# A gated cross-attention block: what follows the attention on groups of 128 rows across batches

## What is computed

```python
def xattn(hidden, ctx, mask, ...):            # per batch: hidden 100x256, ctx 1444x256
    q, k, v = hidden @ Wq.T + bq, ctx @ Wk.T + bk, ctx @ Wv.T + bv   # 16 heads of 16
    scores = clip(q @ k.T / 4, -50, 50); scores = where(mask, scores, -50)
    probs = softmax(scores); ctx = probs @ v
    delta = rs * (ctx @ Wo.T + bo)
    return layernorm(delta) * gamma + beta

def ffn(x, w1, w2, w3):                       # aq: rows to 8 bits, wq: weights to -1, 0, 1
    h = silu(aq(x) @ wq(w1).T) * (aq(x) @ wq(w2).T)
    return aq(h) @ wq(w3).T

x = x + tanh(g_xattn) * xattn(layernorm(x), ctx_2048, mask, ...)
x = x + tanh(g_ffn) * ffn(layernorm(x), w1, w2, w3)
```

## Time and profile before

| | us |
|---|---|
| median of 3 runs | 1345.64 (1344.66 to 1347.27) |
| the profiled execution's own span | 1347.5 |
| TensorE busy in it | 1303.3 |
| VectorE | 1114.3 |
| ScalarE | 964.8 |
| GpSimd | 443.3 |
| one batch in the middle | 40.0 |

### The profile page before, as it was taken

The page is one execution under the profiler, slowest core; times in us unless marked ns, Lnnn a source line. Parts: engine busy times, 40 slices in busy tenths (PEclk is TensorE's granted clock), DMA queues, the critical chain, the costliest instruction groups (busy, mean ns, idle before and its releaser), DMA issues.

```text
span 1347.5 us, 48025 instructions
## 1 busy us (share of the span) xinstructions
PE 1303.3 (97%) x19984; PEld 1207.4 (90%) x19984; DVE 1114.3 (83%) x2248; ACT 964.8 (72%) x1617; POOL 443.3 (33%) x751
## 2 busy tenths in 40 slices
PE   5999999999999999999999999999999999999993
PEld 4988999999999999999999999999999999999982
DVE  5878888888888888888888888888888888888864
ACT  3776777677777777777777777767777777777761
POOL 3323333323334322333332334332333332333310
PEclk9999999999999999999999999999999999999985
DMA  8867677667777767777767767766767776767630
GB/s 227 195 154 169 162 187 169 161 166 171 164 185 174 166 164 168 173 169 178 168 164 174 173 157 187 173 162 164 174 154 191 172 166 165 173 165 177 148 74 9
DMA packets 142511, 222.15 MB, mean 165 GB/s; under 512 B 29194, under 2 KB 135630, under 8 KB 142286
## 3 DMA queue, kind: packets, MB, share of 16 engines
q1 hardware_dynamic: 128632, 198.78, 61.3%
q0 software_dynamic: 12288, 19.69, 6.7%
q10 hardware_dynamic: 1366, 0.53, 0.2%
HBM read 54.00 MB, written 3.28 MB: 43 GB/s over the span
## 4 chain that ended last, share of the span: by engine, by line
PE 89%; SPq 4%; DVE 3%; DMA 2%; issue 1%; ACT 1%; POOL 0%; DVEq 0%; POOLq 0%
PE sc L1239 22%; PE pvb L1259 20%; PE cb L1294 19%; PE cb L1280 18%; SPq L309 4%; PE mb L1351 3%; PE mb L1320 2%; PE mb L1329 2%; DMA k_st<-k_lo 2%; PE mb L1366 2%; PE mb L1358 1%; DMA c_in<-in_ctxT 0%; PE mb L1313 0%; DVE c_hi L754 0%; PE mb L1335 0%
## 5 line engine op out<-in xcount | busy, mean ns | idle before, releaser
L556 ACT ACTIVATE e_sb<-sc 121x800 f32<-121x800 f32 (+1 forms) x768 | 645.6, 847 | 147.9 <-PE sc L1239 135.3
L1239 PE MATMUL sc<-q_st,k_st 96*121 96x200 f32 (+1 forms) x3072 | 472.2, 276 | 7.1 <-issue 3.0
L1239 PEld LDWEIGHTS sc<-q_st,k_st 96*121 96x121 f32 (+1 forms) x3072 | 411.6, 185 | 34.6 <-issue 8.5
L793 DVE TENSOR_SCALAR e_sb<-e_sb,hi_b 121x1600 f32<-121x1600 f32 (+1 forms) x384 | 399.6, 1048 | 0.8 <-ACT e_sb L556 0.8
L1259 PE MATMUL pvb<-e_sb,v_sb 121*32 121x100 f32 x12288 | 287.6, 251 | 0.0
L1259 PEld LDWEIGHTS pvb<-e_sb,v_sb 121*32 121x32 f32 x12288 | 266.3, 110 | 22.2 <-issue 19.0
L1294 PE MATMUL cb<-wv_hi,c_hi 128*121 128x256 f32 (+1 forms) x768 | 222.1, 289 | 1.6 <-DVE k_lo L784 1.3
L784 DVE SCALAR_TENSOR_TENSOR k_lo<-cb,bk_c,k_hi 128x484 fp32r<-128x484 f32 (+1 forms) x192 | 134.5, 700 | 107.5 <-ACT k_hi L568 107.5
L1294 PE MATMUL cb<-wv_hi,c_lo 128*121 128x256 f32 (+1 forms) x768 | 216.1, 281 | 0.0
L1294 PE MATMUL cb<-wv_lo,c_hi 128*121 128x256 f32 (+1 forms) x768 | 216.0, 281 | 0.0
L470 POOL DMA_DIRECT2D q_st<-bd_hi x256 | 164.0, 644 | 123.7 <-DVE bd_lo L839 120.7
(11 more groups left out here) (160 smaller groups left out, 1508.5 us busy)
## 6 DMA issues: line engine op xcount, KB each, us to landing
k_st<-k_hi SPq DMA_DIRECT2D x512, 121.0 KB, 2.9
c_in<-in_ctxT SPq DMA_DIRECT2D x64, 484.0 KB, 4.0
k_st<-k_lo SPq DMA_DIRECT2D x256, 121.0 KB, 2.9
k_st<-k_hi SPq DMA_DIRECT2D x256, 119.0 KB, 3.5
c_in<-in_ctxT SPq DMA_DIRECT2D x32, 476.0 KB, 4.7
k_st<-k_lo SPq DMA_DIRECT2D x128, 119.0 KB, 3.2
q_st<-bd_hi POOLq DMA_DIRECT2D x256, 50.0 KB, 3.3
q_st<-bd_lo POOLq DMA_DIRECT2D x128, 50.0 KB, 3.3
```

The source lines that it names most:

```text
L556: nc.scalar.activation(e_sb[e_slot(b, n)][0:TL[n], k * SW:(k + 1) * SW].rearrange("p (o c) -> p o c", o=2), sc[q % NSC][0:TL[n], :, 0:2 * PW],
L793: V.tensor_scalar(e, e, E_LO, hi_b[b.par][0:TL[n], n:n + 1], ALU.max, ALU.min).then_inc(clip_done, 1)
L1239: last = T_.matmul(sc[q % NSC][0:TL[n], e // 2, (e % 2) * PW:(e % 2 + 1) * PW], k_st[st_slot(b, n // TPC)][:, pr // NQ, pr % NQ, t0:t0 + T ...
```

## The change

The rows of all batches are taken as one array of 3200 rows, cut into 25 groups of 128. `full_group(b)` gives the group whose last rows are batch b's, or nothing for the seven batches that complete none. The softmax division of each batch writes its 100 columns of oT into a ring of 256 columns (in two pieces where they wrap); the first half of the attention's reading goes to a tile pT of its own. Every step behind that (`delta` to `result`) runs once per group, at the tile at which it ran before, in the batch behind the one that completes the group, on 128 partitions, with `gd` and `ge` in place of the batches d and b-2. x_res gets its 128 rows by a load of its own from x (`load_res`, SP's queue), and beta is added in place by GpSimd. The transposes of x2 and h read 128 rows. The count of steps of the attention's own part moves to a new semaphore (`A_V`). `load_x` waits for xn instead of the addition of beta. The general pass is written out batch by batch in place of its hardware loops.

The core of the diff; renamed or widened tiles of the same kind, the general pass's calls and repeated forms are left out:

```diff
+    NG = NB * S // P
+    RING = 2 * P
...
-        x_res = [sb(f"x_res{i}", [S, H]) for i in range(2)]
+        x_res = [sb(f"x_res{i}", [P, H]) for i in range(2)]
...
-        zt, oT = sb("zt", [P, KT, S]), sb("oT", [P, KT, S])
+        zt, pT, oT = sb("zt", [P, KT, S]), sb("pT", [P, KT, S]), sb("oT", [P, KT, RING])
...
+        def full_group(b):
+
+            g = S * (b.row + 1) // P - 1
+            if b.row < 0 or g < S * b.row // P:
+                return None
+            return whole(g, NG if b.base else 0)
...
+        def ring(row, count):
+
+            start = row % RING
+            first = min(count, RING - start)
+            return [(0, slice(start, start + first))] + ([(first, slice(0, count - first))] if first < count else [])
+
+        x_rows, out_rows = x.rearrange("b s h -> (b s) h"), out.rearrange("b s h -> (b s) h")
...
-            def store(b):
-                sp.wait_ge(result_done, b.n + 1)
-                sp.dma_start(out[bass.ds(b.row, 1), :, :].rearrange("o s h -> (o s) h"), y_out[:, :]).then_inc(stored, 16)
+            def store(g):
+                sp.wait_ge(result_done, g.n + 1)
+                sp.dma_start(out_rows[P * g.row:P * (g.row + 1), :], y_out[:, :]).then_inc(stored, 16)
+
+            def load_res(g):
+                if g.row >= 2:
+                    sp.wait_ge(dve_post, D_V.after(g.plus(-2), "x1"))
+                elif g.base:
+                    sp.wait_ge(dve_post, D_V.after(whole(NG - 1), "x1"))
+                sp.dma_start(x_res[g.par][:, :], x_rows[P * g.row:P * (g.row + 1), :]).then_inc(res_loaded[g.par], 16)
...
                 if nxt2:
-                    sp.wait_ge(pool_x, X_P.after(b, "res"))
+                    sp.wait_ge(dve_x, X_V.after(b, "xn"))
                     load_x(b.plus(2))
+                if full_group(b):
+                    load_res(full_group(b))
                 if nxt:
                     sp.wait_ge(split_done, SPLIT.after(b.plus(1), "lo0"))
                     load_c(b.plus(1), 2)
-                if prev2:
-                    store(b.plus(-2))
+                if full_group(b.plus(-2)):
+                    store(full_group(b.plus(-2)))
                 stack_k(b, 2)
...
+            def residual(g):
+                pool.wait_ge(res_loaded[g.par], res_count(g))
+                if not g.base and g.row == 0:
                     pool.wait_ge(s_setv, SETV["beta"])
-                if older:
-                    pool.wait_ge(dve_post, D_V.after(b.plus(-2), "x1"))
-                nc.gpsimd.tensor_tensor(x_res[b.par][:, :], x_in[b.par][:, :], beta_t[0:S, :], ALU.add
-                                        ).then_inc(pool_x, 1)
+                alone()
+                nc.gpsimd.tensor_tensor(x_res[g.par][:, :], x_res[g.par][:, :], beta_t[:, :], ALU.add
+                                        ).then_inc(pool_res, 1)
...
             def attention_out(b):
-                d_wait(b, "rz")
-                dv(V.tensor_tensor(oT[:, :, :], oT[:, :, :], zs[:, :, :], ALU.mult))
+                a_wait(b, "rz")
+                for at, cols in ring(S * b.row, S):
+                    size = cols.stop - cols.start
+                    put = V.tensor_tensor(oT[:, :, cols], pT[:, :, at:at + size], zs[:, :, at:at + size], ALU.mult)
+                av(put)
...
-            def x_turn(b, user):
+            def x_turn(b, user, older):
                 pe.wait_ge(dve_x, X_V.after(b, "xn"))
                 if user:
                     pe.wait_ge(dve_post, D_V.after(user, "dl"))
+                elif older:
+                    pe.wait_ge(result_done, older.n + 1)
...
-                for k in range(KT):
-                    last = T_.matmul(mb[0:S, 0:H], oT[:, k, :], wo[:, k, :], start=k == 0, stop=k == KT - 1)
+                cols = slice(P * g.row % RING, P * g.row % RING + P)
                 for k in range(KT):
+                    last = T_.matmul(mb[:, 0:H], oT[:, k, cols], wo[:, k, :], start=k == 0, stop=k == KT - 1)
                 last.then_inc(pe_post, 1)
...
                 for k in range(KT):
-                    last = T_.transpose(mb16[:, k * S:(k + 1) * S], x2q[:, k * P:(k + 1) * P], identb[0:S, 0:S])
+                    last = T_.transpose(mb16[:, k * P:(k + 1) * P], x2q[:, k * P:(k + 1) * P], identb[:, :])
...
                 for k in range(FT):
-                    last = T_.transpose(mb16[:, k * S:(k + 1) * S], hq[:, k * P:(k + 1) * P], identb[0:S, 0:S])
+                    last = T_.transpose(mb16[:, k * P:(k + 1) * P], hq[:, k * P:(k + 1) * P], identb[:, :])
...
-                    if prev2 and n == 2:
-                        down(b.plus(-2))
+                    if ge and n == 2:
+                        down(ge)
                     if nxt:
                         if n == 4:
-                            x_turn(c, d if prev else None)
+                            x_turn(c, gd, ge)
                         if n == 5:
                             x_query(c)
-                    if prev:
+                    if gd:
                         if n == 3:
-                            delta(d, prev2)
+                            delta(gd, d)
...
-                            x2_turn(d)
+                            x2_turn(gd)
                         if n == 8:
-                            up(d, 0, 0)
+                            up(gd, 0, 0)
                         if n in (9, 10):
-                            up(d, n - 9, 1)
+                            up(gd, n - 9, 1)
                     attend()
-                    if prev2 and n == 1:
-                        h_turn(b.plus(-2))
-                    if prev and n == 9:
-                        up(d, 1, 0)
+                    if ge and n == 1:
+                        h_turn(ge)
+                    if gd and n == 9:
+                        up(gd, 1, 0)
```

More of the change, by code:

```diff
@@ L207, in flamingo_block @@
         stored = sem("stored")
+        res_loaded = [sem(f"res_loaded{i}") for i in range(2)]
+        pool_res, dve_att = sem("pool_res"), sem("dve_att")
         odd_known, care_known = sem("odd_known"), sem("care_known")
@@ L335, in _, with batch @@
             sp.dma_start(m_in[0:TL[-1], NT - 1, :], maskT[(NT - 1) * TT:T, :]).then_inc(s_mask, 16)
-            def batch(b, own, nxt, nxt2, prev2):
+            def batch(b, own, nxt, nxt2):
                 if own:
@@ L1188, in passes @@
                 for step in (first_sum, x1_stats, x1_aggr):
-                    step(e)
+                    step(last)
                 if not base:
@@ L1365, in down, with batch @@
                 for k in range(FT):
-                    last = T_.matmul(mb[0:S, 0:H], hT[:, k, :], w3q[:, k, :], start=k == 0, stop=k == FT - 1)
+                    last = T_.matmul(mb[:, 0:H], hT[:, k, :], w3q[:, k, :], start=k == 0, stop=k == FT - 1)
                 last.then_inc(pe_post, 1)
-            def batch(b, own, nxt, prev, prev2):
+            def batch(b, own, nxt, prev):
                 c, d = b.plus(1), b.plus(-1)
+                gd, ge = full_group(d), full_group(b.plus(-2))
                 first = not prev
@@ L1442, in passes @@
                         ctx_item(b, w, 1)
-                batch(whole(0, base), True, True, False, False)
-                batch(whole(1, base), True, True, True, False)
-                batch(whole(2, base), True, True, True, True)
-                if base:
-                    with pe.Fori(base // 2 + 1, (base + NB - 2) // 2) as i:
-                        batch(Batch(2 * i + 1, i, 1, base), True, True, True, True)
-                        batch(Batch(2 * i + 2, i + 1, 0, base), True, True, True, True)
-                else:
-                    for n in range(3, NB - 1):
-                        batch(whole(n), True, True, True, True)
+                for n in range(NB - 1):
+                    batch(whole(n, base), True, True, n > 0)
                 e = whole(NB - 1, base)
-                batch(e, True, False, True, True)
+                batch(e, True, False, True)
+                last = full_group(e)
                 for n in range(NT - VISIT, NT):
@@ L1457, in passes @@
                     pv(e, n, 1)
-                h_turn(e.plus(-1))
-                down(e.plus(-1))
-                delta(e, True)
+                h_turn(last.plus(-1))
+                down(last.plus(-1))
+                delta(last, e)
                 if not base:
```

325 lines of the change are left out of this document (151 added, 174 removed).

## The result

The changed kernel takes **1331.9 us** (median of four runs, 1329.4 to 1335.6), the kernel before 1346.0 beside it: a ratio of 0.990 with a 95% interval of 0.988 to 0.992. The profiled execution was the fastest of the four, 1329.4 us with a span of 1327.6 (a run's time is 1.8 us more than its span in every run here).

A forecast was written before the change was run, and what follows sets the result against it. The order of TensorE's instructions was taken to set the time. -21.0 + 2.4 + 0.4 + 2.5 + 0.5 + 2.8 = -12.4 us took the profiled 1347.5 to 1335.1, the median to 1333.2 us; range 1327 to 1340.

The forecast's parts named there:

- -21.0, what leaves TensorE: TensorE steps missing in the two batches behind each of seven that complete no group: 3.00 us per batch, -21.0 in all.
- +2.4, the wider turns: The eight turns per group on TensorE go from 100 to 128 moving columns: 0.10 us a group, +2.4 us.
- +0.4, the last group: In the last group, where all is in series, the wider turns and copies cost some +0.4 us.
- +0.5, the wrapped ring: Twelve batches whose columns wrap the 256-column ring get a second VectorE multiplication: +0.5 us (0 to 1.5).
- (1) +2.5, VectorE's list in b+2: Two batches behind each gap, TensorE waits 0.36 us for VectorE's k_lo before tile 7's v product: +2.5 us (0 to 6.2).
- (2) +2.8, the stacking of k in b+1: One batch behind each gap, TensorE waits 0.4 us for k_st copies before tile 0's scores: +2.8 us (0 to 8.0).
- rival B: No new stalls, as k_lo, q_st and copies may come earlier: 1327.4 us; sign: b+1 falls to 37.9; chance 0.20.
- The offset: The profiled execution stands 1.9 us over the runs' median (1345.64), so 1335.1 becomes a median of 1333.2 us.
- Rival A: The forecast itself, with its stalls between half and double: 1329 to 1338 us; chance 0.60.
- D: Rival: 25 extra 128 KB x_res loads delay the k_st copies in every group's batch: slower, 1350 us; chance 0.05.
- E: Rival: TensorE's stationary-column loads are no longer hidden, 10 us on top of the forecast: 1343 us, no change; chance 0.04.

The follow-up runs named there:

- Run 1: Changed kernel with TensorE repeating the missing group steps, unread, in six of seven places; other engines as in the changed kernel: 1349.5 us, ratio 1.0045 to the kernel before.
- run 8: Changed kernel without VectorE's 1.40 us reciprocal of the softmax sums in the seven batches b+2: 1329.7 us, ratio 0.9897 to the kernel before.
- run 5: Changed kernel with the turns of x2 and h and ScalarE's copies of them back at 100 rows and columns: 1331.8 us, ratio 0.9903.
- run 6: Changed kernel with the last six of twelve copies of each batch's first key chunk issued by GpSimd instead of SyncE: 1536.1 us, ratio 1.143.
- run 9: Changed kernel without the body of the general pass, flag still read: 1330.8 us, ratio 0.989 to the kernel before.
- run 10: Changed kernel with GpSimd issuing the eight rounded-part query copies first, the four of the remainder behind them: 1325.8 us, ratio 0.9852.
- run 3: Changed kernel with queries (q_st) copied for the first two batches only, later batches using old q: 1328.2 us, ratio 0.9877.
- run 11: Kernel before, with only GpSimd's rounded-part query copies issued first and the remainder's behind them: 1339.2 us, ratio 0.9953.
- the clean pair: Traces of the kernel before and the changed kernel, both with rounded query copies issued first, on one chip: medians 1339.2 and 1326.9 us.
- run 4: Changed kernel without 23 of the 25 x_res loads, beta added to what is there: 1333.3 us, ratio 0.9926.
- run 7: Changed kernel with GpSimd's d_ve, d_rstd and d_r made for 100 of the 128 rows: 1335.2 us in its one run.
- run 2: Changed kernel with the third key chunk's remainder made ahead of VectorE's reciprocal, in all batches: 1344.2 us, ratio 1.0005 to the kernel before.

## Why the prediction was right

The forecast was 1333.2 us and rested on seven times 3.00 us of TensorE less what comes back. The median is 1331.9, and the mechanism held: what leaves TensorE sets the gain, and part of it comes back at two waits. That the number came out within 1.3 us is partly luck, as the sum of the steps at the end shows. By its own steps:

- **-21.0, what leaves TensorE.** Right in size. Run 1 puts the work back and takes the gain away. In b+1 the forecast was 2.11 and 40.0 to 37.9 is 2.1; in b+2 it was 0.89, and without the reciprocal's stall (run 8) b+2 falls 0.9 below 40.0.
- **+2.4, the wider turns.** The group batches grew by 0.1 us as forecast, and the turns hold 0.09 of it in the chain of waits (0.07 of h, 0.02 of x2); run 5 takes back 0.05 to 0.09. The down projection's 0.02 was not in the sum.
- **+0.4, the last group.** Not to be told: from the first score of batch 30 on it is 111.4 us before and 110.9 after, and 110.1 to 112.3 in the experiments (runs 6 and 9 aside), which is more scatter than 0.4.
- **+0.5, the wrapped ring.** Not seen: batches whose columns wrap are no longer than the others.
- **(1) +2.5, VectorE's list in b+2. The size was about right, the place wrong.** I put the stall at the value product of tile 7, where the slack was 0.14. There the slack is 0.3 to 0.4 in the b+2 of now, and 0.5 to 0.6 in the group batches. The stall came earlier, at tile 3, behind the reciprocal: 2.8 us in all. In the kernel before the slack there was 0.67 us, so 0.89 - 0.67 = 0.22 is waited for, and the load that is then not hidden adds 0.25. The failing step was to take the chain with the least slack in one batch of before as the one that would give. In b+2 everything ahead of tile 3 that leaves (turn of h, down) leaves TensorE, so that the product there arrives the full 0.9 us earlier, while the reciprocal's list starts no earlier than the attention products end. I should have tabulated the slack of every product that waits for VectorE, not of one. Why tile 7 has more slack now was not tested.
- **(2) +2.8, the stacking of k in b+1. Mis-sized; it measured about 0.6 us in the six b+1 from batch 5 on.** b+1 was forecast at 38.3 and is 37.9, which the prediction named as the mark of rival B. The assumed slack was right: its median over batches 3 to 31 is 0.78 us before. TensorE does come 1.1 us sooner: from the scores of tile 7 to those of the next tile 0 it is 12.5 us in b+1 for 13.6. And the chunk is only just in time, with 0.04 to 0.4 us to spare behind the six b+1 from batch 5 on. What failed is the step that held the landing of the copies fixed while TensorE came sooner. In these b+1 the last copy landed 12.5 us behind tile 7's scores for 12.8 before (medians), and they last 0 to 0.2 us longer than in run 10, where the chunk has time to spare. The query copies set out together with the key copies there, and 0.7 us behind them before; that this is the reason, as rival B had it, wasn't tested alone. Over all batches the copies are late more often (slack at 0.1 or less in 11 batches for 5), but the sum over the long batches went from 3.9 to 3.5 us: that scatter is in both kernels and goes with the query copies (runs 3, 10 and 11).
- **The offset.** The 1.9 us set a span (1347.5) against a median of times, which are 1.8 us more than spans; by the same measure the profiled execution of before stood some 3.6 us above the median. The forecast isn't touched, since the sum is taken off either. With 3 us in the head and 1 to 3 in late chunks, a profiled execution can stand that far to either side, as the one of after does (2.5 below).
- **Rival A's band.** Half and double of the stalls (2.5 + 0.5 + 2.8) give 1330 to 1339, not 1329 to 1338; nothing hangs on it.

In the batches the forecast's terms make -21.0 + 2.4 + 0.5 + 2.5 + 2.8 = -12.8. The first pair of traces has -16.5 there and the clean pair -15.9, while the medians lie 14.1 and 12.3 apart. So the forecast met the medians, and the traces say that it gave back some 3 us too much, which is about term (2) and the ring; the 2 to 4 us between traces and medians stay open, and without them the forecast would have been 3 us off. D and E are refuted: the loads of x_res cost nothing (run 4), and six products with 128 stationary columns take 0.67 for 0.65. Nor did the loads of stationary columns all grow, as E had it. Those of the down projection, before and after (count, busy us, mean ns):

```profile
L1366 PEld LDWEIGHTS mb<-w3q,hT 128*100 128x100 bf16 x192 | 22.0, 126 | 1.9 <-ACT hT L616 1.9
...
L1382 PEld LDWEIGHTS mb<-w3q,hT 128*128 128x128 bf16 x150 | 12.9, 99 | 4.7 <-ACT hT L632 2.2
```

With 28 more columns each bf16 load got shorter, 99 ns for 126, and so did those of the ups (99 for 124). Those for Wo, in fp32, got longer: 189 ns for 170.

The Trainium skill (TensorE: Matmul & The Clock Gate, section LDWEIGHTS (loading the stationary operand)) puts a load at its columns/1.2 in ns, so by an estimate from it 128 columns take 23 ns more than 100. The fp32 loads agree in size (19 ns more); the bf16 loads don't, they fell by 27, and there the measurement decides.

## What to carry to other kernels

Where one engine's order sets the time, work taken off it counts in full until the next product meets its operand: so list the slack of *every* wait on that engine, by batch, before pricing what comes back. A remainder queued behind a long instruction can't be moved ahead for free if what waits for that instruction has less slack than the remainder takes. And before a scatter in the periods is put down to a change, look for it in the kernel before; here it led to a change of order in one loop, worth 5 to 7 us beside the 14 of the change.

## What the runs showed of the hardware

**A small GpSimd instruction beside a VectorE instruction can take about a microsecond longer, and which of two it is differs between the kernels.** In the kernel before, the first step of the chain to d_r overlapped VectorE's clip (1.05 us) and took 1373 ns; the groups of GpSimd by line (count, busy us, mean ns):

```profile
L441 POOL TENSOR_SCALAR d_ve<-dmv,scal 100x1 f32<-100x1 f32 x32 | 43.9, 1373 | 433.5 <-DVE dmv L889 433.5
...
L444 POOL TENSOR_TENSOR d_rstd<-d_ve,minus_half 100x1 f32<-100x1 f32 x32 | 17.6, 549 | 2.7
```

In the changed kernel the first is short and the second, which now overlaps the same clip, is long:

```profile
L466 POOL TENSOR_TENSOR d_rstd<-d_ve,minus_half 128x1 f32<-128x1 f32 x25 | 28.4, 1137 | 2.1
...
L463 POOL TENSOR_SCALAR d_ve<-dmv,scal 128x1 f32<-128x1 f32 x25 | 10.9, 438 | 344.2 <-DVE dmv L907 344.2
```

That makes the first sum start 0.35 us sooner behind the aggregate, and may be where tile 7's slack comes from; this link was not tested. The Trainium skill (SBUF — State Buffer, section Who interferes with whom) has a port pair that VectorE and GpSimd take in turn, each for a whole instruction. That one of two GpSimd steps is long beside the clip fits that, but d_ve starts 0.40 and the clip 0.62 us behind the start of the aggregate in both kernels, so the order of issue doesn't explain the difference, and run 7 excludes the partition count of GpSimd's steps, not that of VectorE's. The cause is open.

**A long stall of TensorE costs one and a half times to twice its length.** In run 6 the granted clock was 0.50 for some 4 us behind the stall at tile 0 of batch 12, and over the whole run 4.4 us of stall a batch cost 6.7. In run 9 batch 2 began with a stall of 3.9 us for the key chunk; the stretch of the stall and the next two:

```profile
108.00:112.10 4.10, 0.21 (x3) 0.04 (x2) 2.85 (x4) 0.87 (x2) 0.49 (x1) 0.96 0.94 239
112.10:116.00 3.90, 3.90 (x14) 3.56 (x15) 0.00 (x0) 1.58 (x2) 0.00 (x0) 0.50 0.89 201
116.00:120.00 4.00, 4.00 (x81) 3.27 (x83) 1.69 (x3) 1.59 (x3) 0.00 (x0) 0.68 0.32 88
```

That batch 2 lasted 42.7 us instead of 39.6, so that 3.9 us of stall cost 7.0. Behind 2.99 us in run 2 the clock was 0.50 over the next 3.8 us, behind 2.25 us in run 7 it was 0.58 over 4, and batch 2 lasted 43.0 and 41.3. Behind shorter stalls it stayed at 1.00: 0.98 and 1.39 us in the changed kernel, 1.78 in run 5, 2.11 ahead of batch 1 in run 7. So a first chunk as late as that of batch 2 in runs 2, 7 and 9 weighs more than its stall, and one as late as in the changed kernel doesn't. It may be part of the scatter between executions that I had called noise; for executions without a profile only the total is known.
